# Neighbourhood attention on one core: normalising and projecting one step later, projection jobs inside the step

## The reference, cut to what matters

```python
qkv = (x @ qkv_w + qkv_b).reshape(B, H, W, 3, HEADS, HEAD_DIM)     # 4 heads of 32
q = qkv[..., 0, :, :] * HEAD_DIM ** (-0.5); kk = qkv[..., 1, :, :]; v = qkv[..., 2, :, :]
kwin = kk at the 7 x 7 window of each pixel (shifted inward at the border); vwin likewise
scores = einsum('bxyhd,bxyklhd->bxyhkl', q, kwin) + bias
attn = softmax(scores over the 49 neighbours)
out = einsum('bxyhkl,bxyklhd->bxyhd', attn, vwin).reshape(B, H, W, C)
attn_out = out @ proj_w + proj_b
gate = sigmoid(relu(x @ g1_w + g1_b) @ g2_w + g2_b)
x = attn_out * gate + x
```

## Time and profile before

| | |
|---|---|
| time, median of 3 runs | 4601.78 us |
| the profiled execution | 4611.34 us, span 4609.5 us |
| PE busy | 3873.8 us (84%) |
| PE weight loads | 2996.1 us (65%) |
| DVE busy | 3406.9 us (74%) |
| ACT busy | 2678.2 us (58%) |
| POOL busy | 1391.3 us (30%) |
| layer 0 | 0 to about 798 us |
| data moved in layer 0, 100 to 760 us | 198 GB/s |

### The profile page before, as it was taken

The page is one execution under the profiler, slowest core; times in us unless marked ns, Lnnn a source line. Parts: engine busy times, 40 slices in busy tenths (PEclk is TensorE's granted clock), DMA queues, the critical chain, the costliest instruction groups (busy, mean ns, idle before and its releaser), DMA issues. The chain is left out here.

```text
span 4609.5 us, 73934 instructions
## 1 busy us (share of the span) xinstructions
PE 3873.8 (84%) x25590; PEld 2996.1 (65%) x25590; DVE 3406.9 (74%) x7889; ACT 2678.2 (58%) x6018; POOL 1391.3 (30%) x1373
## 2 busy tenths in 40 slices
PE   6888887799999999999999999676999644455579
PEld 4666665699988998899888998444666311111148
DVE  4666666577787777777787777695666798899934
ACT  3666665577776777767776667333222466666621
POOL 2434443100010000200010000112244599999910
PEclk9999999799999999999999999898999755555579
DMA  7777774200010000100010000212222311122143
GB/s 205 204 199 198 197 198 137 76 24 21 18 37 27 20 24 16 42 24 24 17 39 13 10 10 10 67 62 95 77 77 71 145 55 55 60 69 71 58 151 102
DMA packets 274687, 346.40 MB, mean 75 GB/s; under 512 B 34954, under 2 KB 159754, under 8 KB 272778
## 3 DMA queue, kind: packets, MB, share of 16 engines
q1 hardware_dynamic: 261738, 320.55, 22.8%
q0 software_dynamic: 12288, 16.92, 1.4%
q10 hardware_dynamic: 288, 4.19, 0.2%
HBM read 209.58 MB, written 130.02 MB: 74 GB/s over the span
## 5 line engine op out<-in xcount | busy, mean ns | idle before, releaser
L864 ACT ACTIVATE l_ph<-l_T 128x512 fp32r<-128x512 f32 x1024 | 612.4, 598 | 547.2 <-PE l_T L777 547.2
L974 DVE TENSOR_TENSOR l_pl<-l_T,l_ph 128x512 fp32r<-128x512 f32 x1024 | 707.3, 691 | 274.9 <-ACT l_ph L864 274.2
L963 DVE CUSTOM_DVE_ANT_0 l_pr<-l_S,l_zero 128x512 f32<-128x512 f32 x1024 | 704.7, 689 | 74.1 <-PE l_S L700 11.2
L869 ACT ACTIVATE l_pr<-l_pr,l_st 128x512 f32<-128x512 f32 x1024 | 731.5, 714 | 1.1 <-DVE l_st L969 1.0
L789 PE MATMUL l_O<-l_ph,l_vh 128*128 128x256 f32 x2048 | 661.7, 323 | 12.2 <-DVE l_pl L974 12.1
L777 PE MATMUL l_T<-l_ident,l_pr 128*128 128x128 f32 x4096 | 612.8, 272 | 0.0
L777 PEld LDWEIGHTS l_T<-l_ident,l_pr 128*128 128x128 f32 x4096 | 507.6, 140 | 136.2
L790 PE MATMUL l_O<-l_ph,l_vl 128*128 128x256 f32 x2048 | 577.9, 282 | 0.0
L791 PE MATMUL l_O<-l_pl,l_vh 128*128 128x256 f32 x2048 | 576.8, 282 | 0.0
L1005 POOL TENSOR_TENSOR l_xs<-l_xs,l_bob 128x128 f32<-128x128 f32 x128 | 57.1, 461 | 1644.7 <-DMA l_xs<-x 1643.6
L1658 PE MATMUL l3b_C<-l_D,l_sel 32*128 32x512 f32 x256 | 216.4, 845 | 384.5 <-DVE l3b_E L1716 384.1
(11 more groups left out here) (241 smaller groups left out, 8842.7 us busy)
## 6 DMA issues: line engine op xcount, KB each, us to landing
hls<-l_hl SPq DMA_DIRECT2D x64, 512.0 KB, 4.7
l_qs<-hls SPq DMA_DIRECT2D x96, 256.0 KB, 3.8
l_ks<-hls SPq DMA_DIRECT2D x96, 256.0 KB, 4.0
l_xc<-x1t SPq DMA_DIRECT2D x64, 256.0 KB, 2.7
zs<-l3a_tmp SPq DMA_DIRECT2D x64, 256.0 KB, 2.0
l3b_z<-zs SPq DMA_DIRECT2D x64, 256.0 KB, 2.8
yz<-l3b_z SPq DMA_DIRECT2D x64, 256.0 KB, 2.0
l3c_y<-yz SPq DMA_DIRECT2D x16, 1024.0 KB, 17.1
```

The costliest lines, as they stand in the source:

```text
L864: e.activation(ph[:, i, :], psT[:, i, :], ACT.Copy).then_inc(p_hi, 1)
L869: e.activation(pr[:, s, es], pr[:, s, es], ACT.Exp, bias=st[:, s, 9:10], scale=SC, accum_out=st[:, s, 10 + k:11 + k]).then_inc(exped, 1)
L963: e.tensor_tensor_reduce(pr[:, s, ks], psS[:, bk, :], zero[:].broadcast_to([128, 512]), 1.0, -3.0e38, ALU.add, ALU.max, st[:, s, kc:kc + 1 ...
L974: e.tensor_tensor(pl[:, i, :], psT[:, i, :], f32(ph[:, i, :]), ALU.subtract).then_inc(p_lo, 1)
```

## The change

Three things move; no instruction is added but the loop's last turn.

- `normalise`, the output projection, `finish` and the store of `ys` work on tile n-5 (the store on n-6) where they worked on n-4 (n-5). R is made for tile n-4 in place of n-3, behind `attend(n-3)` as before, and waits for `finish` of tile n-5. The loop has one step more, N + 7.
- The jobs k, q, v and hide stay at the head of the step on PE. On ACT they come behind head 0's exp and copy, on DVE behind head 1's score, copy and `invert`.
- open is a list of its own (`openings`), in the same step as before. PE does it behind head 2, ACT at the end of the step, DVE at the head of the next.

```diff
@@ -131,16 +131,16 @@
         def jobs(n):
 
             G, i = n // 4 + 2, n % 4
-            out = []
-            if i == 0 and 2 < G <= NB:
-                out.append(("open", G - 1))
-            if G < NB:
-                out.append((("k", "q", "v", "hide")[i], G))
-            return out
+            return [(("k", "q", "v", "hide")[i], G)] if G < NB else []
+
+        def openings(n):
+
+            G, i = n // 4 + 1, n % 4
+            return [("open", G)] if i == 0 and 2 <= G < NB else []
 
         before = [(what, G) for G in range(2) for what in ("q", "k", "v", "hide", "open")]
         p_use, hi_use = {}, {}
-        for job in before + [j for n in range(N + 6) for j in jobs(n)]:
+        for job in before + [j for n in range(N + 7) for j in jobs(n) + openings(n)]:
             p_use[job] = len(p_use)
             if job[0] in ("q", "k"):
                 hi_use[job] = len(hi_use)
@@ -222,7 +222,7 @@
                 keep_v(G)
                 fetch(G + 2)
             bring(0)
-            for n in range(N + 6):
+            for n in range(N + 7):
                 if n == 2:
                     bias(1)
                 elif n == 12:
@@ -258,13 +258,13 @@
                 e.tensor_tensor(xs[:, n % 7, :], xs[:, n % 7, :], tg[:, n % 2, :], ALU.add).then_inc(based, 1)
 
             bring(0)
-            for n in range(N + 6):
+            for n in range(N + 7):
                 if 0 <= n - 2 < N:
                     base(n - 2)
-                if 0 <= n - 5 < N:
-                    b, r0, c0, _, _ = where(n - 5)
-                    w.wait_ge(y_done, n - 4)
-                    e.dma_start(x1[b, r0:r0 + 8, c0:c0 + 16, :], ys[:, (n - 5) % 3, :]).then_inc(y_out[(n - 5) % 3], 16)
+                if 0 <= n - 6 < N:
+                    b, r0, c0, _, _ = where(n - 6)
+                    w.wait_ge(y_done, n - 5)
+                    e.dma_start(x1[b, r0:r0 + 8, c0:c0 + 16, :], ys[:, n % 3, :]).then_inc(y_out[n % 3], 16)
                 if n + 1 < N:
                     bring(n + 1)
             for i in range(3):
@@ -345,16 +345,20 @@
                         score(n, h)
                     if 0 <= n - 2 < N:
                         turn(n - 2, h)
-                    if h == 1 and 0 <= n - 4 < N:
-                        w.wait_ge(normed, n - 3)
-                        e.matmul(psF[:, 128:256], ot[:, n % 2, :], wp[:], start=True, stop=True).then_inc(Y_full, 1)
+                    if h == 1 and 0 <= n - 5 < N:
+                        w.wait_ge(normed, n - 4)
+                        e.matmul(psF[:, 128:256], ot[:, (n - 5) % 2, :], wp[:], start=True, stop=True).then_inc(Y_full, 1)
+                    if h == 2:
+                        for what, G in openings(n):
+                            project(what, G)
                 if 0 <= n - 3 < N:
                     attend(n - 3)
-                    w.wait_ge(summed, n - 2)
-                    if n >= 4:
-                        w.wait_ge(y_done, n - 3)
+                if 0 <= n - 4 < N:
+                    w.wait_ge(summed, n - 3)
+                    if n >= 5:
+                        w.wait_ge(y_done, n - 4)
                     for h in range(4):
-                        t = e.matmul(psF[32 * h:32 * h + 32, 0:128], st[:, (n - 3) % 4, 12 + h:13 + h].broadcast_to([128, 32]), ident[:],
+                        t = e.matmul(psF[32 * h:32 * h + 32, 0:128], st[:, n % 4, 12 + h:13 + h].broadcast_to([128, 32]), ident[:],
                                      start=True, stop=True, tile_position=(0, 32 * h))
                     t.then_inc(R_full, 1)
 
@@ -379,9 +383,7 @@
 
             for what, G in before:
                 project(what, G)
-            for n in range(N + 6):
-                for what, G in jobs(n):
-                    project(what, G)
+            for n in range(N + 7):
                 if 0 <= n - 4 < N:
                     w.wait_ge(attended, n - 3)
                     if n >= 6:
@@ -397,6 +399,11 @@
                         if n >= 4:
                             w.wait_ge(attended, n - 3)
                         e.activation(ptb[0:110, n % 2, h, :], psT[0:110, 0, 0:384], ACT.Copy).then_inc(T_even, 1)
+                    if h == 0:
+                        for what, G in jobs(n):
+                            project(what, G)
+                for what, G in openings(n):
+                    project(what, G)
 
         def vector(e):
             w = Waits(e)
@@ -462,8 +469,8 @@
             e.tensor_scalar(cols[:, 4:5], cols[:, 4:5], -1.0, None, ALU.mult).then_inc(prepared, 1)
             for what, G in before:
                 project(what, G)
-            for n in range(N + 6):
-                for what, G in jobs(n):
+            for n in range(N + 7):
+                for what, G in openings(n - 1):
                     project(what, G)
                 for h in range(4):
                     if n < N:
@@ -473,12 +480,15 @@
                         if n >= 4:
                             w.wait_ge(attended, n - 3)
                         e.tensor_copy(ptb[0:110, n % 2, h, :], psT[0:110, 1, 0:384]).then_inc(T_odd, 1)
-                    if h == 0 and 0 <= n - 4 < N:
-                        normalise(n - 4)
+                    if h == 0 and 0 <= n - 5 < N:
+                        normalise(n - 5)
                     if h == 1 and 0 <= n - 2 < N:
                         invert(n - 2)
-                    if h == 2 and 0 <= n - 4 < N:
-                        finish(n - 4)
+                    if h == 1:
+                        for what, G in jobs(n):
+                            project(what, G)
+                    if h == 2 and 0 <= n - 5 < N:
+                        finish(n - 5)
 
         P.run(sync, tensor, scalar, vector, gpsimd)
```

## The result

The changed kernel takes 4623.58 us (median of 5 runs, 4619.85 to 4628.1) where the kernel before takes 4602.1 us (5 runs, 4601.56 to 4609.4): a ratio of 1.0043, 95% interval 1.0029 to 1.0058. A second comparison gave 4622.85 against 4604.22 us, 1.0044 (1.0031 to 1.0057). Forecast were 4603.8 us and "no difference"; the time lies outside the range of 4588 to 4616.

The account below looks back on a forecast made before the run. The prediction took SP's queue to bound layer 0 up to attend(118). Its terms, 0 + 0 + 0 + 2.0 us, brought the profiled 4611.34 to 4613.3 and the median 4601.78 to 4603.8 us; range 4588 to 4616.

Parts of the forecast that it names:

- What bounds the kernel: Layer 0 up to attend(118): SP's queue sets the period, 23.28 us a group, against 22.63 for the engines' loop.
- (1) Moved jobs: Layer 0's q and k steps: engines' loop gains 1.5 to 2.8 us a group, worth 0 on SP's path.
- (2): Gate's last product (open) apart, on PE behind head 2 in layer 0: cost 0.
- (3): P_free and SP's k or q write later within a step, closest at n = 4: bound 0 to +1 us, taken 0.
- (4) The delay: Normalising, projecting, finishing one step later: free in layer 0's steady part, one more round at its end, +2.0 us (+1 to +3).
- SP's k writes still 23.3 us apart: Sign in the profile after: SP's period per group of four steps in layer 0 stays at 23.3 us.
- attend(118) within 3 us of 759.7: Sign in the profile after: attend(118), near layer 0's end, starts within 3 us of 759.7.
- those on PE's waits: Signs in layer 0: wait for `ot` at L350 nearly gone; waits for V windows and k from 11.3 to over 40 us.
- the last round: Sign at the end of layer 0: one more round of 2 us.
- Rival B: SP's landings in layer 0 change by 0.3 us each, 17 us: shorter 4587 (chance 0.06), longer 4620 at most (0.05).
- Rival A: SP is not layer 0's bound; the period follows the engines' loop: 55 to 87 us saved, 4549 to 4517; chance 0.09.
- Rival C: Layer 0: early PE stands still, falls to the low clock: +15 us, 4619, at the far end +30, 4634; chance 0.10.

Follow-up runs that it names:

- e3: Kernel before, with SP issuing the step's V window between the write of q or k and the wait for its landing: 4587.68 us, ratio 0.9941.
- e4: Changed kernel, with SP issuing the step's V window between the write of q or k and the wait for its landing: 4543.03 us, ratio 0.9851.
- e2: Kernel before with only the jobs moved inside the step and open apart, normalising left at tile n-4: ratio 1.0001.
- e13: Second run of the kernel before with only the jobs moved inside the step and open apart, without the delay: ratio 1.0006.
- e8: Kernel before with moved jobs and open apart, no delay, and SP's V window issued inside the landing: ratio 0.9843.
- e14: Second run of the kernel before with only normalising, projecting and finishing one step later, jobs as before: ratio 1.0031.
- e17: Changed kernel with SP's V window issued inside the landing, run again beside e18: 4550.74 us, ratio 0.9870 to the kernel before.
- e18: Moved jobs without the delay, with SP's V window issued inside the landing, run beside e17: 4534.56 us, ratio 0.9835 to the kernel before.
- e7: Kernel before with the delay of one step, jobs as before, and SP's V window issued inside the landing: 4585.20 us, ratio 0.9962.

## Why the prediction was wrong, point by point

**What bounds the kernel**: right. SP's queue is the chain to attend(118); e3 and e4 moved the time by what its period left free.

**(1) Moved jobs, 0 on the path**: right within what can be told. e2 and e13 gave 1.0001 and 1.0006, 0.5 and 3 us. The loop put at 19.8 to 21.1 us measured 20.4 (e8), and all of the gain was hidden, as the 0 said.

**(2) and (3)**: no cost seen. SP wrote k of n = 4 at 77.91 us, no later than before.

**(4) The delay, +2.0 with bounds +1 and +3**: the step that failed. Its mechanism at the end was right: finish(127) is 4.01 us behind attend(127) where it was 2.11, 1.9 us more. (1.3 us came back, as the step behind attend(118) took 3.61 and not 4.92 us, at a granted clock of 1.00 where it was 0.65.) But the delay as a whole measured 11 and 14 us, outside its bounds. The term looked at the steady part for waits between engines (slots that allow the distance, a store that moves by the same step), found none, and took the cost there for nothing; it had no place for transfers that take longer. What the runs show in its place: SP's group went from 23.28 to 23.61 us (23.11 to 23.54 in the second pair), with the waits for landings 10.0 and 11.5 us longer over 25 groups. So the signs "SP's k writes still 23.3 us apart" and "attend(118) within 3 us of 759.7" did not come (23.61; 766.66), while those on PE's waits and on the last round did.

**Rival B, longer landings**: this is what happened, and it was given 0.05 because "the transfers are the same". They are, in number and bytes. The sum of landings grew by 10.0 and 11.5 us all the same, over half of the 17 us that the rival's 0.3 us on each would have made. In the first pair of profiles layer 0 grew by 7.6 us: -0.9 up to n = 16, 8.3 over the 25 groups, 0.2 behind them. In the second it grew by 17.8: 4.9, 10.8 and 2.1 us. So the middle part is the landings, and what lies ahead of n = 16 scatters. The median, 4623.58 us, is still 4 us above the rival's "4620 at most". For a chain of which 8.5 us in 23.3 are landings, this had to be a main case, with a price in the range.

**Rival A**: fell. **Rival C**: its mechanism came and its cost didn't, as e2 and e14 show for a loop bound by SP's queue. With SP relieved, e17 against e18, it does show a cost.

**The rule against which the prediction set the trace**: it took PE for the engine that Perfetto Trace Analysis of the Trainium skill (Identifying the Most-Contended Engine) puts first. For the matrix engine that section goes by the weight loads' busy share, not the products'. Over the 25 groups before that is 375.04 of 582.07 us, 64%, and DVE's busy share is 392.45, 67%. So by it DVE comes first, just ahead; that neither was the bound holds either way.

The kernel before was also read from one execution that had layer 0 end 11 us later than a second one. The forecast took over its 9.56 us above the median as a constant, when they were most likely the same scatter of landings.

**What stays open**: why one step of delay lengthens the landings. The phase in which GpSimd issues against SP's writes is, by the timelines, the same with the delay alone as before: in the stretch from 3.5 us ahead of a write until it has landed, GpSimd issues 1.7 to 1.9 stores for a write of k and 1.0 to 1.2 for one of q, with the delay or without. Addresses of x1 are not it. Where the engines are the bound (e3 against e7) the longer landings are there and the profiles show no cost in the steady part. Without GpSimd's loads and stores it is smaller or cannot be told. Which transfer it is that meets which was not found.

## What to carry to other kernels

With a queue that waits for its own transfers to land as the bound, shortening the engines' loop was worth nothing here, and a change that only shifts other DMA traffic cost 11 to 14 us: price each landing on the chain with both signs. The remedy is to put independent issues of the same queue inside the landing; a few lines of reordering here were worth 0.6% alone and 1.6% with the moved jobs. And when a change has two parts of which one makes the loop shorter, measure them apart: here the jobs are the gain and the delay is only a cost.

## What the runs showed of the hardware that was not expected

GpSimd's loads of 64 KB a step are 256 KB of some 4.6 MB that a group moves (198 GB/s over 23.3 us), 6%. Leaving them out takes 30 us, 13%, off 238 us of landings on another queue, 0.4 us for each of the 75 landings; leaving out the stores, as many bytes, takes 12 us. The Trainium skill (DMA: Bandwidth & Descriptors, Issuing engines are not separate DMA queues) says that transfers of all issuing engines run on the same 16 DMA engines and interleave; the runs agree, and add the price.

A granted clock of 0.93 in place of 0.99 means, by its two levels, PE at half clock for some 12% more of the time (an estimate), and it made 32 us more of busy time in the changed kernel. It cost next to nothing, since PE was not the bound (e2: 0.93 and a ratio of 1.0001). With PE 96% busy, 0.98 in place of 1.00 came with 10.5 us more of PE's work in a stretch that was 14.7 us longer (e17, e18).
